# The first product of an attention kernel taken piece by piece over all row tiles, with joint query and key transfers and sixteen transposes ahead of it

## The chip, the cores and the metric

The kernel runs on one core of one Trainium2 chip, alone. The metric is the time of one execution in microseconds (us) as the device measures it; a kernel's time is the median of several executions. Lower is better.

## The reference, cut to what matters

The input x is (4, 512, 512) in float32. A first layer computes single-head attention over each of the four sequences, an MLP on its result and a second MLP on the result and the first MLP's output together; three further layers are adapters with weights chosen per sequence by an index, each with a residual and a layer norm. Only the attention is near the change:

```python
q = x @ Wq
k = x @ Wk
v = x @ Wv
attn = jnp.einsum('btd,bTd->btT', q, k) * scale
attn = jax.nn.softmax(attn, axis=-1)
attn_out = jnp.einsum('btT,bTd->btd', attn, v) @ Wp + bp
cms_out = jax.nn.gelu(attn_out @ cW1 + cb1, approximate=False) @ cW2 + cb2
```

## The kernel before, in words

**Arithmetic.** Each float32 operand is split into two parts for TensorE: a high part, which ScalarE makes by a cast to `fp32r`, and a low part, which VectorE makes by subtracting the high part from the operand. A product of two operands is then three matmuls (high by high, high by low, low by high) that accumulate in one PSUM bank: `mm3` (line 538). Its matmuls all stand on line 541 in the profile. Tiles are 128 rows; a 512 by 512 by 512 product has four row tiles `m` and four pieces `k` of the contraction, so 4 x 4 x 3 = 48 matmuls of 128x128 by 128x512, and each row tile has a PSUM bank of its own. `product` (line 545) goes over `m` outside and `k` inside; in the first row tile it calls `ready(k)`, which waits for the semaphore of piece `k`.

**Order of the work.** The kernel does not compute q and k. It forms G = Wq Wk^T once (`J_G`, into `g_w`) and for each sequence U = G x^T (`J_U0`, then per sequence), and scores from U and x. Likewise Wv Wp is formed once (`J_VP`). TensorE's program (lines 583 to 604) is: `J_G` in the upper four banks (`HIGH`), `J_U0` in the lower four (`LOW`), `J_VP` in the upper, `J_S0` (scores of sequence 0) in the lower; then for each sequence values (`v_jobs`), transposes of the probabilities (`pT_jobs`, line 572, by the identity in `ident`), probabilities by values, and U and scores of the next sequence. After that come the up and down products of the two MLPs (from line 606 on) and the three adapter layers.

**Loads at the front.** SyncE issues all transfers here (lines 364 to 375), in this order: for each `k` the query rows into `wq_raw` and the key rows into `wk_raw` (256 KB each, a semaphore each, line 366), x of sequence 0 into `res` (1 MB), the value and projection weights (1 MB each), four small ones, and the expert indices, whose values it then waits for and reads before it goes on (line 376).

**The splits at the front.** ScalarE (lines 809 to 812) waits for one transfer after the other and casts it into the high part of `wqT` or `wkT` (semaphore `qk_hi`); VectorE (lines 1127 to 1130) makes the low parts in the same order (`qk_split`). After the eight pieces ScalarE casts x, copies the four banks of `J_G` into the high parts of `g_w` as they fill (line 773) and casts the value and projection weights; VectorE makes the low parts in the same order (line 1072 for `g_w`), and then sums the betas of the later layers (`bsum`, line 1139).

**The prep pieces.** A second job goes along with the attention: the adapter weights (36 pieces) are loaded into three slots `prep`, cast by ScalarE (`piece_hi`, line 788, at places written out by hand between its other work), subtracted by GpSimd (line 1498) and stored in DRAM by SyncE (lines 389 to 404). In the first phase SyncE issues two loads and then waits for the sum of the betas (`bsum_store`, line 382) before the first store and the third load. The cast of the last piece of the first phase stands on ScalarE ahead of the exponentials of sequence 0 (line 793), and the first values of `v_jobs` wait for an exponential to release a bank.

**The identity.** GpSimd makes it at the start (lines 1483 to 1486); TensorE waits for it on line 590, after four products.

Of the kernel before, what the change touches and what calls it, by code (L numbers as in the profile page):

```python
# [8 lines left out]
ALU = mybir.AluOpType  # L9
# [3 lines left out]
P = 128  # L13
B = 4
S = 512
V = 512
# [4 lines left out]
DT = V // P  # L21
# [32 lines left out]
NRAW = 3  # L54
DSTEP = 8
GHL = 3


def chunk_of(ci):
# [36 lines left out]
    return tuple(n + LAYER_STEPS[l].index((i, part)) for i in (P4, P3))  # L96


def build(nc, wts, xin, bias_in, codes_in, experts_in, up_w, dn_w, wdu_all, pp_all, gb_all,
          bup_all, out):  # L100
    ctx = ExitStack()
    with ctx:
        base = -(-nc.sbuf_base // 64) * 64

        def at(name, kib, shape, dt=F32):

            return nc.alloc_sbuf_tensor_at(name, shape, dt, offset=base + int(kib * KiB))

        def sem(name):
            return ctx.enter_context(nc.semaphore(name))  # L110

        wqT = at("wqT", 0, [P, 2, DT, V], F32R)
        wkT = at("wkT", 16, [P, 2, DT, V], F32R)
# [7 lines left out]
        pT = at("pT", 144, [P, 2, DT, S], F32R)  # L121
        wp_s = at("wp_s", 144, [P, 2, DT, V], F32R)

        wq_raw, wk_raw, wv_raw, wp_raw = (at(f"w{n}_raw", 112 + 8 * i, [P, DT, V]) for i, n in enumerate("qkvp"))

        res = at("res", 160, [P, B, DT, S])
        probs = at("probs", 192, [P, DT, S])
# [10 lines left out]
        g = at("g", 128, [P, QC, 4, S])  # L138
        g_hl = [at(f"g_hl{i}", 144 + 4 * i, [P, 2, S], F32R) for i in range(GHL)]
        u_t, v_t, w_t = (at(n, k, [P, S]) for n, k in (("u_t", 156), ("v_t", 158), ("w_t", 204)))  # L140
# [15 lines left out]
        ident = at("ident", 206, [P, P])  # L156
        sm = at("sm", 206.5, [P, 224])
        NB_BIAS = 2 * HT + 3 * DT
        bias = sm[:, 0:NB_BIAS]
# [31 lines left out]
        bank = [psum[:, i, :] for i in range(BANKS)]  # L191
# [12 lines left out]
        def f(ap):  # L204

            return ap.bitcast(F32)
# [4 lines left out]
        qk_hi = sem("weights_qk_rows_hi_done")  # L211
        qk_split = sem("weights_qk_rows_split")
        x_hi = sem("x_transposed_hi_done")
        x_split = sem("x_transposed_split")
        s_wqk = [[sem(f"weight_{n}_rows_landed_{i}") for i in range(DT)] for n in ("q", "k")]
        s_x = sem("x_transposed_landed")
        s_small = sem("small_inputs_landed")
        s_idx = sem("experts_landed")
        s_ident = sem("identity_ready")
# [3 lines left out]
        bank_full = sem("bank_full")  # L223
# [78 lines left out]
        LOW, HIGH = 0, DT  # L302
        J_G, J_U0, J_VP, J_S0 = (DT * i for i in range(4))
# [58 lines left out]
        @block.sync  # L362
        def _(sp):
            for k in range(DT):
                for i, w in enumerate((wq_raw, wk_raw)):
                    sp.dma_start(w[:, k, :], wts[2 + i, :, k, :]).then_inc(s_wqk[i][k], 16)
            sp.dma_start(res[:, 0, :, :], xin[0]).then_inc(s_x, 16)
            for i, w in enumerate((wv_raw, wp_raw)):
                sp.dma_start(w[:, :, :], wts[i]).then_inc(s_w[i], 16)
# [19 lines left out]
            for phase in range(B):  # L389
                for c in range(PHASE + 2):  # L390
                    if c >= 2:
                        o = c - 2
                        i = o % PSLOT
                        sp.wait_ge(p_lo, phase * PHASE + (o + 1))
                        sp.dma_start(wdu_split[phase * PHASE + o], prep[i][:, :, :]).then_inc(p_free[i], 16)
                    if c < PHASE:
                        i = c % PSLOT
# [139 lines left out]
        def _(pe):  # L537
# [7 lines left out]
            def product(n, group, lhs, rhs, ready=None, free=None, tiles=range(DT)):  # L545

                for m in tiles:
                    if free is not None:
                        free(m)
                    elif ready is None or m > 0:  # L550
                        pe.wait_ge(dve_done, n + m - (BANKS - 1))
                    for k in range(DT):
                        if m == 0 and ready is not None:
                            ready(k)
                        ins = mm3(bank[group + m],
                                  lambda e: lhs[:, e, k, m * P:(m + 1) * P], lambda e: rhs[:, e, k, :],
                                  k == 0, k == DT - 1)
                    ins.then_inc(bank_full, 1)

            def split(sem_, before, per_k=1):  # L560

                return lambda k: pe.wait_ge(sem_, before + per_k * (k + 1))
# [17 lines left out]

                return lambda k: pe.wait_ge(dve_done, n + (k + 1) + (1 if k == DT - 1 else 0))

            product(J_G, HIGH, wqT, wkT, ready=split(qk_split, 0, per_k=2), free=known)
            pe.wait_ge(x_split, DT)
            product(J_U0, LOW, g_w, xT, ready=split(dve_done, J_G), free=known)
            pe.wait_ge(s_wsplit[0], 1)
            pe.wait_ge(s_wsplit[1], 1)
            product(J_VP, HIGH, wvT, wp_s)
            product(J_S0, LOW, uT, xT, ready=split(dve_done, J_U0))
            pe.wait_ge(s_ident, 1)  # L590
            for b in range(B - 1):
                n = b * PER
                v_jobs(n + JV, (0, 1, 2), ready=split(dve_done, J_VP))
# [63 lines left out]
            def down_chunk(ci):  # L657
                for d in range(DSTEP):
# [4 lines left out]
                    for m in range(DT):  # L663
                        if k == 0:
                            down_bank_free(ci, q, m)
                        mm3(bank[4 * q + m], lambda e: w_hl[k % 2][:, e, m * P:(m + 1) * P],
                            lambda e: g_hl[(DSTEP * ci + d) % GHL][:, e, :], k == 0, k == 3).then_inc(d_used, 1)

# [98 lines left out]
        def _(act):  # L767
# [39 lines left out]
                nc.scalar.copy((a_ops, c_ops)[s][i][:, 0, :, :], src).then_inc(op_hi[s], 1)  # L807

            for k in range(DT):
                for i, (w, raw_w) in enumerate(((wqT, wq_raw), (wkT, wk_raw))):  # L810
                    act.wait_ge(s_wqk[i][k], 16)
                    nc.scalar.copy(w[:, 0, k, :], raw_w[:, k, :]).then_inc(qk_hi, 1)
            x_hi_parts(0)
            hi_jobs(J_G, HIGH, lambda m: g_w[:, 0, m, :])
            for i, (w, raw_w) in enumerate(((wvT, wv_raw), (wp_s, wp_raw))):
# [8 lines left out]
            for b in range(B - 1):  # L824
                n = b * PER
# [84 lines left out]
            def g_hi(ci, d):  # L910
# [4 lines left out]
                if t >= GHL:  # L915
                    act.wait_ge(d_used, 4 * (t - GHL + 1))
                nc.scalar.copy(g_hl[t % GHL][:, 0, :], g[:, q, 2 * row + seq, :]).then_inc(g_hi_done, 1)  # L917

# [48 lines left out]
            for ci in range(NCH):  # L967
                p, l, c = chunk_of(ci)
                for q in range(QC):
                    for pos in range(len(LAYER_STEPS[l])):  # L970
                        n = aop_at(ci, q) + pos
# [94 lines left out]
        def _(dve):  # L1066
# [58 lines left out]
                    nc.vector.tensor_tensor((a_t4, c_t4)[s][:, :, :], b21, b11, ALU.subtract).then_inc(t_sum[s], 1)  # L1125

            for n in range(2 * DT):
                w, raw_w = ((wqT, wq_raw), (wkT, wk_raw))[n % 2]
                dve.wait_ge(qk_hi, n + 1)
                nc.vector.tensor_tensor(w[:, 1, n // 2, :], raw_w[:, n // 2, :], f(w[:, 0, n // 2, :]), ALU.subtract).then_inc(qk_split, 1)  # L1130
            x_lo_parts(0)
            lo_jobs(J_G, HIGH, g_w)
            for i, (w, raw_w) in enumerate(((wvT, wv_raw), (wp_s, wp_raw))):
# [18 lines left out]
            for b in range(B - 1):  # L1152
                n = b * PER
# [177 lines left out]
            for ci in range(NCH):  # L1331
                p, l, c = chunk_of(ci)
                for q in range(QC):
                    for pos in range(len(LAYER_STEPS[l])):
                        n = aop_at(ci, q) + pos
# [248 lines left out]
```

## Time and profile before

| | us |
|---|---|
| median of 3 runs | 1236.32 |
| lowest and highest run | 1235.46, 1237.90 |
| the profiled execution's own time | 1239.01 |
| its span, from the first instruction to the last | 1236.9 |
| TensorE busy in the span | 1191.9 |
| VectorE, ScalarE, GpSimd busy | 807.4, 567.0, 173.5 |
| mean granted TensorE clock in the span | 0.994 |

The span is the part of an execution that the profile shows instruction by instruction; what lies around it is in the execution's own time alone. Busy times of engines overlap. Ends of matmuls are modelled, so that spacings from start to start say more than durations. The row PEclk has the granted clock in tenths of full speed (9 stands for 90% or more); in a table by stretches it is a share of 1.00.

### The profile page before, as it was taken

What the parts mean: (1) busy time and instruction counts of PE and PEld (TensorE: products, weight loads), DVE (VectorE), ACT (ScalarE), POOL (GpSimd) and SP (SyncE); (2) the same over time, 40 slices, a digit from 0 to 9 for tenths busy, and PEclk for the clock granted to TensorE, in tenths of its full rate; (3) what the DMA queues carried; (4) which work ended last, traced back from release to release, by engine and by line L of the source; (5) the groups of instructions that cost most, each with busy time, mean ns of one, the idle gap of its engine ahead of it and who ended that gap; (6) DMA issues with size and microseconds to landing.
All of it is one profiled execution on the core that took longest, in us unless ns stands there. A gap on an engine that the chain in (4) does not pass through costs nothing.

```text
span 1236.9 us, 15228 instructions
## 1 busy us (share of the span) xinstructions
PE 1191.9 (96%) x5312; PEld 973.7 (79%) x5312; DVE 807.4 (65%) x1461; ACT 567.0 (46%) x1068; POOL 173.5 (14%) x147
## 2 busy tenths in 40 slices
PE   7999999799999899999999999989999999999997
PEld 5878878677788688888887787768888888788776
DVE  5444385746766766565766666686665565879986
ACT  5334353554533534343524633544343433266666
POOL 1332230000000000000000000000000000488871
PEclk9999999899999999999999999999999999999999
DMA  5755452114312202020461221411111118655534
GB/s 189 271 199 180 162 176 85 43 43 153 122 58 77 87 16 94 10 94 9 169 274 51 88 83 51 171 51 51 52 52 52 52 34 322 229 189 193 175 137 170
DMA packets 51186, 145.82 MB, mean 118 GB/s; under 512 B 6420, under 2 KB 6420, under 8 KB 46886
## 3 DMA queue, kind: packets, MB, share of 16 engines
q1 hardware_dynamic: 51110, 144.84, 33.2%
q8 instruction: 43, 0.70, 0.2%
q14 instruction: 33, 0.27, 0.1%
HBM read 108.11 MB, written 36.71 MB: 117 GB/s over the span
## 4 chain that ended last, share of the span: by engine, by line
PE 71%; DVE 11%; POOL 8%; ACT 4%; issue 4%; DMA 1%; SPq 0%; POOLq 0%; DVEq 0%; ACTq 0%
PE psum L541 70%; POOL res L1525 3%; POOL res L1527 3%; DVE ring L1187 1%; DMA prep<-wdu_dram 1%; ACT z L1016 1%; ACT ring L877 1%; POOL sm L1518 1%; DVE g_hl L1254 1%; DVE sm L1434 1%; DVE res L1269 1%; DVE res L1324 1%; DVE w_t L1228 0%; DMA wk_raw<-wts_dram 0%; POOL prep L1498 0%
## 5 line engine op out<-in xcount | busy, mean ns | idle before, releaser
L541 PE MATMUL psum<-g_hl,w_hl 128*128 128x512 f32 x1536 | 353.3, 390 | 1.5 <-DVE g L1242 1.3
L541 PE MATMUL psum<-a_op,ring 128*128 128x512 f32 x1344 | 324.4, 394 | 17.5 <-DVE w_t L1228 11.1
L541 PEld LDWEIGHTS psum<-g_hl,w_hl 128*128 128x128 f32 x1536 | 287.9, 188 | 64.6 <-DVE g L1242 4.8
L541 PEld LDWEIGHTS psum<-a_op,ring 128*128 128x128 f32 x1344 | 252.9, 190 | 77.8 <-DVE w_t L1228 14.5
L541 PE MATMUL psum<-c_op,ring 128*128 128x512 f32 x672 | 166.1, 394 | 0.6 <-DVE c_op L1296 0.6
L1254 DVE TENSOR_TENSOR g_hl<-g,g_hl 128x512 fp32r<-128x512 f32 x128 | 87.7, 691 | 111.7 <-ACT g_hl L917 110.4
L541 PEld LDWEIGHTS psum<-c_op,ring 128*128 128x128 f32 x672 | 127.3, 190 | 28.5 <-DVE c_op L1296 2.0
L1506 POOL TENSOR_TENSOR yT<-res,yT 128x512 fp32r<-128x512 f32 x8 | 11.7, 1487 | 875.6 <-ACT yT L1011 875.6
L877 ACT CAST ring<-asum 128x256 fp32r<-128x256 f32 x192 | 76.2, 403 | 122.3 <-PE psum L541 100.9
L917 ACT CAST g_hl<-g 128x512 fp32r<-128x512 f32 x128 | 78.3, 618 | 101.1 <-PE psum L541 101.1
L1187 DVE TENSOR_TENSOR ring<-asum,ring 128x256 fp32r<-128x256 f32 x192 | 80.8, 422 | 63.8 <-ACT ring L877 61.3
L894 ACT ACTIVATE g<-g,sm 128x512 f32<-128x512 f32 x96 | 69.6, 725 | 109.9 <-DVE g L1234 47.5
L1187 DVE TENSOR_TENSOR ring<-rawp,ring 128x256 fp32r<-128x256 f32 x144 | 60.8, 422 | 81.0 <-ACT ring L877 81.0
L1269 DVE TENSOR_TENSOR res<-psum,res 128x512 f32<-128x512 f32 x96 | 64.8, 691 | 24.1 <-PE psum L541 24.0
L877 ACT CAST ring<-rawp 128x256 fp32r<-128x256 f32 x144 | 57.0, 403 | 46.3 <-PE psum L541 46.2
L541 PE MATMUL psum<-yT,wd 128*128 128x512 f32 x288 | 68.6, 394 | 6.0 <-issue 6.0
L1498 POOL TENSOR_TENSOR prep<-prep 128x512 f32<-128x512 f32 x36 | 51.6, 1437 | 131.4 <-ACT prep L788 131.4
L541 PE MATMUL psum<-wu,h_hl 128*128 128x512 f32 x288 | 67.4, 390 | 0.0
L541 PEld LDWEIGHTS psum<-yT,wd 128*128 128x128 f32 x288 | 53.1, 188 | 18.0 <-issue 7.3
L541 PEld LDWEIGHTS psum<-wu,h_hl 128*128 128x128 f32 x288 | 54.0, 188 | 11.2
L1016 ACT ACTIVATE z<-z,sm 128x512 f32<-128x512 f32 x46 | 33.9, 808 | 37.7 <-DVE sm L1402 37.7
L1525 POOL TENSOR_TENSOR res<-z,bc 128x512 f32<-128x512 f32 x32 | 48.2, 1507 | 12.4 <-ACT z L1016 12.4
(124 smaller groups left out, 1381.2 us busy)
## 6 DMA issues: line engine op xcount, KB each, us to landing
rawp<-up_w_dram SPq DMA_DIRECT2D x48, 512.0 KB, 3.6
wdu_split<-prep SPq DMA_DIRECT2D x36, 512.0 KB, 2.9
wraw<-dn_w_dram SPq DMA_DIRECT2D x64, 256.0 KB, 3.1
wd<-wdu_split SPq DMA_DIRECT2D x12, 1024.0 KB, 7.3
wu<-wdu_split SPq DMA_DIRECT2D x12, 1024.0 KB, 5.4
prep<-wdu_dram SPq DMA_DIRECT2D x36, 256.0 KB, 3.3
second_pair_operands<-c_op SPq DMA_DIRECT2D x7, 1024.0 KB, 6.9
a_op<-second_pair_operands SPq DMA_DIRECT2D x7, 1024.0 KB, 11.3
```

What stands on the lines that cost most here:

```text
L541: ins = nc.tensor.matmul(ps, lw(el), rw(er), start=first and i == 0, stop=last and i == 2, skip_group_check=skip)
L877: nc.scalar.copy(ring[n % RING][:, 0, :], aop_src(n)).then_inc(aop_hi, 1)
L894: nc.scalar.activation(dst, src, ACT.Gelu, bias=(cb1, mb1)[l][:, t:t + 1]).then_inc(gelu_done, 1)
L917: nc.scalar.copy(g_hl[t % GHL][:, 0, :], g[:, q, 2 * row + seq, :]).then_inc(g_hi_done, 1)
L1016: nc.scalar.activation(z[u % 2][:, i, :], z[u % 2][:, i, :], ACT.Identity, scale=rstd[:, u % 2, i:i + 1], bias=nmr[:, u % 2, i:i + 1]).the ...
L1187: nc.vector.tensor_tensor(ring[n % RING][:, 1, :], aop_src(n), f(ring[n % RING][:, 0, :]), ALU.subtract).then_inc(aop_lo, 1)
L1254: nc.vector.tensor_tensor(g_hl[t % GHL][:, 1, :], g[:, q, 2 * row + seq, :], f(g_hl[t % GHL][:, 0, :]), ALU.subtract).then_inc(g_lo_done, 1)
L1269: nc.vector.tensor_tensor(dst, bank[4 * seq + m], dst, ALU.add).then_inc(d_evac, 1)
L1324: nc.vector.tensor_scalar(res[:, 2 + seq, m, :], res[:, 2 + seq, m, :], 0.0, 1.0, ALU.max, ALU.min).then_inc(y0_done, 1)
L1498: nc.gpsimd.tensor_tensor(prep[i][:, 1, :], prep[i][:, 1, :], prep[i][:, 0, :], ALU.subtract).then_inc(p_lo, 1)
L1525: nc.gpsimd.tensor_tensor(res[:, u % B, i, :], z[i2][:, i, :], bc[i2][:, 0, :], ALU.mult).then_inc(t_rmul, 1)
L1527: nc.gpsimd.tensor_tensor(res[:, u % B, i, :], res[:, u % B, i, :], bc[i2][:, 1, :], ALU.add).then_inc(t_res, 1)
```

## The change

In SyncE's program the eight transfers of query and key rows become four: piece `k` of both goes into `wqk_raw[:, k]`, whose layout in DRAM and in SBUF is partition, query or key, 512 values, so that 4 KB of a partition are contiguous. There is one semaphore per piece. ScalarE waits once per piece and casts the query part and then the key part; VectorE's subtractions read the new tile.

On TensorE the first product has a function of its own, `product_by_pieces`. It goes over `k` outside and `m` inside: for each piece it waits for both high parts, does the high by high matmul of all four row tiles, waits for both low parts, and does the two mixed matmuls of all four. The 48 matmuls are the same and write the same four banks. Ahead of it TensorE waits for the identity and transposes it sixteen times (`WARM`) into bank 0, which `J_U0` later overwrites. The wait for the identity further down is gone.

```diff
         def _(sp):
             for k in range(DT):
-                for i, w in enumerate((wq_raw, wk_raw)):
-                    sp.dma_start(w[:, k, :], wts[2 + i, :, k, :]).then_inc(s_wqk[i][k], 16)
+                sp.dma_start(wqk_raw[:, k, :, :], wqk[k]).then_inc(s_wqk[k], 16)
             sp.dma_start(res[:, 0, :, :], xin[0]).then_inc(s_x, 16)
...
-            product(J_G, HIGH, wqT, wkT, ready=split(qk_split, 0, per_k=2), free=known)
+            def product_by_pieces():
+
+                for k in range(DT):
+                    pe.wait_ge(qk_hi, 2 * k + 2)
+                    for m in range(DT):
+                        nc.tensor.matmul(bank[HIGH + m], wqT[:, 0, k, m * P:(m + 1) * P], wkT[:, 0, k, :], start=k == 0, stop=False)
+                    pe.wait_ge(qk_split, 2 * k + 2)
+                    for m in range(DT):
+                        for el, er in ((0, 1), (1, 0)):
+                            ins = nc.tensor.matmul(bank[HIGH + m], wqT[:, el, k, m * P:(m + 1) * P], wkT[:, er, k, :],
+                                                   start=False, stop=k == DT - 1 and el == 1)
+                        if k == DT - 1:
+                            ins.then_inc(bank_full, 1)
+
+
+            pe.wait_ge(s_ident, 1)
+            for i in range(WARM):
+                nc.tensor.transpose(bank[LOW][:, i % DT * P:(i % DT + 1) * P], ident[:, :], ident[:, :])
+            product_by_pieces()
             pe.wait_ge(x_split, DT)
             product(J_U0, LOW, g_w, xT, ready=split(dve_done, J_G), free=known)
             pe.wait_ge(s_wsplit[0], 1)
             pe.wait_ge(s_wsplit[1], 1)
             product(J_VP, HIGH, wvT, wp_s)
             product(J_S0, LOW, uT, xT, ready=split(dve_done, J_U0))
-            pe.wait_ge(s_ident, 1)
...
             for k in range(DT):
-                for i, (w, raw_w) in enumerate(((wqT, wq_raw), (wkT, wk_raw))):
-                    act.wait_ge(s_wqk[i][k], 16)
-                    nc.scalar.copy(w[:, 0, k, :], raw_w[:, k, :]).then_inc(qk_hi, 1)
+                act.wait_ge(s_wqk[k], 16)
+                for i, w in enumerate((wqT, wkT)):
+                    nc.scalar.copy(w[:, 0, k, :], wqk_raw[:, k, i, :]).then_inc(qk_hi, 1)
...
             for n in range(2 * DT):
-                w, raw_w = ((wqT, wq_raw), (wkT, wk_raw))[n % 2]
+                w = (wqT, wkT)[n % 2]
                 dve.wait_ge(qk_hi, n + 1)
-                nc.vector.tensor_tensor(w[:, 1, n // 2, :], raw_w[:, n // 2, :], f(w[:, 0, n // 2, :]), ALU.subtract).then_inc(qk_split, 1)
+                nc.vector.tensor_tensor(w[:, 1, n // 2, :], wqk_raw[:, n // 2, n % 2, :], f(w[:, 0, n // 2, :]), ALU.subtract).then_inc(qk_split, 1)
```

## Rows read from the trace of the kernel before

**Rows 1.** The page: TensorE's busy time, the granted clock in 40 slices, the chain.

```profile
PE 1191.9 (96%) x5312; PEld 973.7 (79%) x5312; DVE 807.4 (65%) x1461; ACT 567.0 (46%) x1068; POOL 173.5 (14%) x147
...
PEclk9999999899999999999999999999999999999999
...
PE 71%; DVE 11%; POOL 8%; ACT 4%; issue 4%; DMA 1%; SPq 0%; POOLq 0%; DVEq 0%; ACTq 0%
```

**Rows 2.** The chain in order of time, 0 to 60 us: start, duration, what.

```profile
3.07 5.98 DMA wk_raw<-wts_dram
...
10.47 47.09 PE psum L541 x198
```

**Rows 3.** Timeline, the first two products: start, duration, engine, line, operation, count, idle before.

```profile
6.23 1.65 PE L541 MATMUL psum<-wkT,wqT 128*128 128x512 f32 x3 [6.23 <-DVE wkT L1130]
...
10.47 11.71 PE L541 MATMUL psum<-wkT,wqT 128*128 128x512 f32 x42 [0.74 <-DVE wkT L1130]
...
22.02 11.04 PE L541 MATMUL psum<-xT,g_w 128*128 128x512 f32 x48
```

**Rows 4.** Stretches: length, PE, PEld, DVE, ACT, POOL, granted clock, DMA share, GB/s.

```profile
239.70:246.40 6.70, 5.51 (x13) 4.34 (x14) 6.21 (x10) 3.74 (x8) 0.00 (x0) 0.50 0.14 42
...
413.80:417.10 3.30, 3.30 (x10) 2.52 (x9) 2.71 (x9) 2.15 (x5) 0.00 (x0) 0.50 0.37 148
...
1229.50:1233.00 3.50, 2.16 (x16) 1.71 (x16) 1.73 (x4) 2.53 (x4) 0.40 (x1) 1.00 0.34 131
```

**Rows 5.** Timeline of TensorE inside two of these stretches.

```profile
240.89 5.49 PE L541 MATMUL psum<-a_op,ring 128*128 128x512 f32 x12 [4.70 <-DVE w_t L1228]
...
414.05 2.76 PE L541 MATMUL psum<-c_op,ring 128*128 128x512 f32 x6
416.61 0.63 PE L541 MATMUL psum<-a_op,ring 128*128 128x512 f32 x1
```

**Rows 6.** Two stretches of the front, columns as in rows 4.

```profile
2.50:8.50 6.00, 2.06 (x4) 1.25 (x5) 2.67 (x4) 3.07 (x5) 0.00 (x0) 1.00 0.93 286
11.00:15.00 4.00, 4.00 (x12) 2.86 (x11) 2.21 (x5) 2.13 (x5) 0.00 (x0) 1.00 1.01 428
```

**Rows 7.** Timeline: the identity and the first piece's splits.

```profile
1.17 0.29 POOL L1485 TENSOR_SCALAR_AFFINE_SELECT ident<-ident 128x128 f32<-128x128 f32 x1 [0.24 <-POOL ident L1483]
...
4.23 0.62 ACT L812 CAST wqT<-wq_raw 128x512 fp32r<-128x512 f32 x1 [2.23 <-DMA wq_raw<-wts_dram]
...
5.49 0.69 DVE L1130 TENSOR_TENSOR wkT<-wk_raw,wkT 128x512 fp32r<-128x512 f32 x1
```

**Rows 8.** Timeline: last tile of `g_w`, sum of betas, first prep pieces; then the page's prep loads.

```profile
21.43 0.83 SPq L399 DMA_DIRECT2D prep<-wdu_dram  x2
22.22 0.59 ACT L773 CAST g_w<-psum 128x512 fp32r<-128x512 f32 x1 [2.13 <-PE psum L541]
...
22.84 0.69 DVE L1072 TENSOR_TENSOR g_w<-psum,g_w 128x512 fp32r<-128x512 f32 x1 [2.03 <-ACT g_w L773]
...
27.51 4.49 POOL L1498 TENSOR_TENSOR prep<-prep 128x512 f32<-128x512 f32 x2 [25.81 <-ACT prep L788]
...
29.06 1.78 DVE L1139 TENSOR_TENSOR bsum<-bsum,bsum 6x512 f32<-6x512 f32 x1
...
prep<-wdu_dram SPq DMA_DIRECT2D x36, 256.0 KB, 3.3
```

**Rows 9.** Timeline: transposes of probabilities, and the last transposes of the kernel.

```profile
62.83 1.91 PE L575 MATMUL psum<-ident,probs 128*128 128x128 f32 x16
...
1231.00 1.75 PE L748 MATMUL psum<-ident,z 128*128 128x128 f32 x14 [0.66 <-ACT z L1016]
```

**Rows 10.** Timeline: where ScalarE's prep casts meet TensorE's stream.

```profile
52.25 0.62 ACT L788 CAST prep<-prep 128x512 fp32r<-128x512 f32 x1 [2.41 <-DMA prep<-wdu_dram]
...
54.66 8.34 PE L541 MATMUL psum<-vp_w,xT 128*128 128x512 f32 x36
...
67.99 11.55 PE L541 MATMUL psum<-pT,v_n 128*128 128x512 f32 x48 [0.50 <-DVE pT L1072]
```

More of the change, by code:

```diff
@@ L56 @@
 GHL = 3
+WARM = 16
 def chunk_of(ci):
@@ L96, in raw_done, with build @@
     return tuple(n + LAYER_STEPS[l].index((i, part)) for i in (P4, P3))
-def build(nc, wts, xin, bias_in, codes_in, experts_in, up_w, dn_w, wdu_all, pp_all, gb_all,
+def build(nc, wqk, wts, xin, bias_in, codes_in, experts_in, up_w, dn_w, wdu_all, pp_all, gb_all,
           bup_all, out):
@@ L122, in build @@
         wp_s = at("wp_s", 144, [P, 2, DT, V], F32R)
-        wq_raw, wk_raw, wv_raw, wp_raw = (at(f"w{n}_raw", 112 + 8 * i, [P, DT, V]) for i, n in enumerate("qkvp"))
+        wqk_raw = at("wqk_raw", 112, [P, DT, 2, V])
+        wv_raw, wp_raw = (at(f"w{n}_raw", 128 + 8 * i, [P, DT, V]) for i, n in enumerate("vp"))
         res = at("res", 160, [P, B, DT, S])
@@ L214, in build @@
         x_split = sem("x_transposed_split")
-        s_wqk = [[sem(f"weight_{n}_rows_landed_{i}") for i in range(DT)] for n in ("q", "k")]
+        s_wqk = [sem(f"weights_qk_rows_landed_{i}") for i in range(DT)]
         s_x = sem("x_transposed_landed")
@@ L1552 @@
     wts = np.stack([rows(a["L0_cond_" + n]) if n == "Wp" else rows(a["L0_cond_" + n].T)
-                    for n in ("Wv", "Wp", "Wq", "Wk")])
+                    for n in ("Wv", "Wp")])
+    wqk = np.stack([a["L0_cond_" + n].T.reshape(DT, P, V) for n in ("Wq", "Wk")], axis=2)
     m_up = np.stack([up_pieces(a["L0_cond_mW1"][:V]), up_pieces(a["L0_cond_mW1"][V:])], axis=1)
@@ L1569 @@
     arrays = {
-        "wts": wts, "x": np.stack([rows(a["x"][b].T) for b in range(B)]), "bias": bias,
+        "wqk": wqk, "wts": wts, "x": np.stack([rows(a["x"][b].T) for b in range(B)]), "bias": bias,
         "codes": a["itok_B_17_1546"].reshape(1, B), "experts": a["itok_B_1_2"].reshape(1, B),
```

## The prediction

> **What bounds the kernel now.** I read the page first: TensorE is busy for 96% of the span, and of the chain that ended last it has 71% [rows 1]. So the kernel is bound by the matmul stream, and a change at the front is worth what it moves the whole stream forward, unless something later takes that back. The chain in order of time says where the front is bound: a transfer of key rows until 9.05 us, a cast, a subtraction, and then 47 us of matmuls without a break from 10.47 [rows 2]. The timeline of TensorE says how those first microseconds look [rows 3]. The first product (48 matmuls) starts at 6.23 with three matmuls, waits, does three more, waits, and is only continuous from 10.47, because the first row tile needs all four pieces before the second tile may start. It ends where the next product (`J_U0`) starts, at 22.02; I call that moment E. The 48 matmuls of that next product take 11.04 us with the longer tail of the last one, 0.227 from one start to the next, 10.9 in all.
>
> **Two speeds.** The first three matmuls take 1.65 us [rows 3], which is what six take at full speed (48 take 11.04). The clock row of the page says 9 from the start, so it can't be used for the first microseconds; I go by spacing. In a stretch with granted clock 0.50 six matmuls start in 2.56 us (414.05 to 416.61), 0.427 each [rows 4, 5]. That is the 1.2 GHz level, 0.227 is the 2.4 GHz level. How long was the slow level at the front? From 10.47 to 22.02 there are 42 matmuls in 11.55 us; at full speed they would take 9.53; the excess of 2.02 is bought at 1 - 0.227/0.427 = 0.47 us per us, so the clock rose some 4 us after the engine had become continuous. The other case in the trace: continuous from 240.89 after an idle time of 4.7 us, and 0.50 until 246.4, so 5.6 us [rows 4, 5]. I use 4 to 5.6 us.
>
> **The change part by part.**
>
> *Transfers.* Eight issues of 256 KB become four of 512 KB, with 4 KB per partition in one stretch where there were 2 KB. In 2.5 to 8.5 us the row pieces moved at 286 GB/s, in 11 to 15 us, with 8 KB stretches, the rate was 428 [rows 6]. For 4 KB I bound by the two and take 350: a piece of 512 KB every 1.5 us (1.83 at the lower rate). The first query piece is in at 4.2, its cast starts at 4.23, and the key piece is in by the end of that cast [rows 7]; so the first joint piece lands between 4.2 and 4.85, I take 4.5. Two casts of 0.62 and a subtraction of 0.69 follow [rows 7]: high parts ready at 4.5 + 1.3 = 5.8, all parts at 6.5. The fourth piece lands at 9.0 (10.3 at the lower rate), its last part is ready at 11.0 (12.3). SyncE issues four fewer transfers of 0.43 us; the x, value and projection rows behind them come up to 1.5 us earlier, or unchanged; neither is waited for (the chain does not go over them).
>
> *The order of the first product.* With pieces outside and row tiles inside, each piece feeds 12 matmuls: 2.7 us at full speed, 5.1 at the slow one. Pieces come every 1.5 to 1.83 us, so after the first piece TensorE never waits. It runs from 5.8 in one go: E = 5.8 + 48 x 0.227 = 16.7 at full speed. The last piece alone would allow 11.0 + 2.7 = 13.7 (15.0 at the late bound), so data don't end last. Each microsecond at the slow clock after 5.8 adds 0.47.
>
> *Price of that order.* All four banks now fill in the last 1.4 us instead of one each 2 to 3 us. Before, three of the four copies and subtractions of `g_w` lay beside matmuls, and only the last showed: cast at 22.22, subtraction at 22.84 [rows 8]. Now ScalarE starts tile 0 at E - 1.2, VectorE ends it at E + 0.1, and then one tile each 0.7 us. The next product needs a new tile each 3 x 0.227 = 0.68 us, so it starts 0.2 late and just keeps pace. The fourth cast starts 0.4 later against E than before and VectorE is free 0.7 later; the weight splits and the sum of the betas (29.06 to 30.84 [rows 8]) stand behind them in order, so I set them 0.5 later against E.
>
> *Transposes of the identity.* The identity is ready at 1.46 [rows 7]. Sixteen transposes of the probabilities take 1.91 us, 0.12 each at full speed [rows 9]. At the slow level no row shows them; an estimate is twice that, 3.8 us, so from 1.5 to 5.3. The first high parts are ready at 5.8, so they cost nothing as such; the cover is 0.5 us, and were it gone each 0.1 us more would put E later by no more than that. The ends of that price: 0.12 each, or 0.80 each if nothing overlapped, as 1.65 us for three matmuls less two spacings leaves 0.80 for a single slow one. I take the estimate, since the nearest row shows transposes overlapped. What they may bring is the clock. If they count as work, the engine is nearly continuous from 1.5, and the clock rises at 5.5 to 7.1: E = 16.7 to 17.3, I take 17.0. If not, it rises 4 to 5.6 after 5.8: E = 18.6 to 19.3, I take 18.9. Do they count? At the end of the kernel, from 1229.5 to 1233, TensorE ran nothing but 16 transposes, 14 of them from 1231.0 on, busy for 2.16 of 3.5 us, and the granted clock of that stretch is 1.00 [rows 4, 9]. That speaks for it, but for holding a clock, not for raising one.
>
> The Trainium skill, "TensorE: Matmul & The Clock Gate", section "Part 4: PE-mode transpose", says the full clock "doesn't engage for transpose-mode". By that rule the sum would take E = 18.9, the first rival below. The rows of the kernel's end lean against it, and none tests it for a rise.
>
> *What follows.* The queue that could hold the rest is that of the `prep` pieces (SyncE load, ScalarE cast, GpSimd subtraction, store). Its stores start when the betas are summed, so it moves by 22.0 - 17.0 - 0.5 = 4.5. Its first two loads are issued at 21.43 [rows 8], behind the value loads of the experts, and come 0 to 1.5 earlier with the transfers. At 0 the first piece lands at 24.7 (3.3 after its issue), is cast in 0.62 and subtracted in some 2.2 (two of them take 4.49 [rows 8]), and the first store could go at 27.5, where it now has to wait for the sum of the betas at 30.84: a shift of 3.3; at 1.5 it would be 4.8, and no bound. I take 4.3, nearer to the second, since the transfers in front of those loads do get shorter. That matters, since this queue touches the stream twice: the cast of the last piece at 52.25 stands ahead of the exponentials that free the banks for 54.66, and the matmuls at 67.99 wait 0.50 for the transposed probabilities behind such a piece [rows 10]. So the gain is that of the queue, 4.3, not the 4.8 of TensorE.
>
> *Sum.* 4.3 us off the profiled execution (1239.0) is 1234.7; its span, 1236.9, is as long as the median of the runs, 1236.3, and the median less 4.3 is 1232.0. A measurement of this kernel can tell about 0.2% (2.5 us) from no change.
>
> **The rivals.** (1) *The transposes don't raise the clock.* E = 18.9, gain 22.0 - 18.9 - 0.5 = 2.6, time 1233.7. For it: no row shows a rise from transposes, and they leave a gap of about 0.5 us before the product. Against it: the clock that held at the end. 0.28. (2) *The piece queue eats it.* If the `prep` loads don't move and each cast then waits for its load, ScalarE, which has the exponentials and the casts of the transposed probabilities behind them, keeps only a part: gain 1 to 2, time 1234.8. For: the zero slack at 67.99. Against: the queue is started anew by the betas, which move with TensorE. 0.15. (3) *The front is bound by data anyway*, the larger transfers landing later or the product waiting for them: gain under 1, time 1235.8. Against: the 3.0 us between 13.7, which the last piece allows, and the 16.7 of 48 matmuls. 0.06. (4) *The transposes hold the first product back.* If they don't overlap in the slow state, 16 x 0.80 = 12.8 puts the product's start at 14.3 and E at 25.2: 3.2 us later, plus 0.5 behind it, time 1240.0. It decides from 0.56 us per transpose (start 10.5, E 21.4). For: no row at this clock. Against: at full speed they overlap, 0.12 each. 0.05.
>
> **How the numbers follow.** Forecast, 4.3: 0.46. Its own range is 3.3 (loads unmoved) to 5.0 (data early, clock up at once), 1231.3 to 1233.0; medians of three lie about 1 us off (the runs spread from 1235.5 to 1237.9). So the low end is 1230.2. Upward rivals 1 and 2 have to be in, with the same 1 us: 1236.4. Faster by over 0.2%: nearly all of the forecast (0.45), over half of rival 1 (0.16), a little of 2 (0.03): 0.64. Slower: rival 4 and 0.02 for a sum of small things: 0.07. Same: 0.29.
>
> **What would show it.** Right: matmuls of the first product in one row of 48 from about 5.8, spacing 0.23 from 7 us or before, the second product starting at 17 to 17.3, and the matmuls now at 54.66 and 67.99 some 4.3 us earlier. Wrong: slow spacing until 10 (rival 1), a longer wait at pT or an exponential behind a cast that waits for a load (rival 2), waits for wkT inside the product (rival 3), transposes beyond 6 us (rival 4). The forecast falls if the shift at 22 us is not found again at the end of the attention.

## The result, and the profile after

The changed kernel takes 1233.14 us (median of 7 runs, 1231.82 to 1235.85); the kernel before, measured beside it, 1238.71 (median of 7, 1235.46 to 1239.85). The ratio is 0.996, with a 95% interval of 0.9946 to 0.9974: about 4.9 us faster, 3.2 to 6.7 by the interval (the two medians lie 5.6 apart). The profiled execution went from 1239.01 to 1233.20 us, its span from 1236.9 to 1231.2.

From the page of the changed kernel: TensorE's busy time is what it was, and it has less of the chain, where VectorE, ScalarE and transfers have more [rows 1].

```profile
PE 1192.0 (97%) x5328; PEld 975.0 (79%) x5328; DVE 806.3 (65%) x1461; ACT 566.3 (46%) x1068; POOL 171.3 (14%) x147
...
PE 68%; DVE 12%; POOL 8%; ACT 5%; issue 3%; DMA 2%; SPq 0%; POOLq 0%; ACTq 0%; DVEq 0%
```

The timeline of the changed kernel's front (start, duration, engine, line, operation, count, idle before):

```profile
1.52 3.33 PE L601 MATMUL psum<-ident 128*128 128x128 f32 x16 [1.52 <-POOL ident L1503]
...
4.42 0.62 ACT L830 CAST wqT<-wqk_raw 128x512 fp32r<-128x512 f32 x1 [2.40 <-DMA wqk_raw<-wqk_dram]
...
5.61 1.20 PE L589 MATMUL psum<-wkT,wqT 128*128 128x512 f32 x4 [0.76 <-ACT wkT L830]
...
6.64 2.02 PE L593 MATMUL psum<-wkT,wqT 128*128 128x512 f32 x8
...
8.50 1.07 PE L589 MATMUL psum<-wkT,wqT 128*128 128x512 f32 x4
...
14.85 1.98 PE L593 MATMUL psum<-wkT,wqT 128*128 128x512 f32 x8
15.51 2.06 ACT L791 CAST g_w<-psum 128x512 fp32r<-128x512 f32 x4 [2.58 <-PE psum L593]
16.12 2.49 DVE L1090 TENSOR_TENSOR g_w<-psum,g_w 128x512 fp32r<-128x512 f32 x4 [2.23 <-ACT g_w L791]
...
16.96 11.13 PE L542 MATMUL psum<-xT,g_w 128*128 128x512 f32 x48
```

Beside rows 3: there the first product began with three matmuls in 1.65 us, at the slow level, and was continuous from 10.47. Here the first four take 1.20, near the 1.07 that four take later at full speed, and from 5.61 there is no further wait; the second product starts at 16.96 where it was 22.02. Sixteen transposes take 3.33 us; spaced 0.213 at first, the last three 0.11 to 0.12 apart, so the clock rose at 4.4 us, while nothing but transposes had run. (The clock column has 1.00 before the first rise in every trace here, so I read every first rise from the spacing of starts.)

Two stretches of the changed kernel, columns as in rows 4: where the pieces land, and one further on.

```profile
4.60:8.00 3.40, 2.64 (x13) 2.00 (x12) 2.93 (x5) 3.13 (x6) 0.00 (x0) 1.00 1.05 428
...
407.20:410.50 3.30, 3.30 (x9) 2.55 (x8) 2.71 (x8) 1.95 (x4) 0.00 (x0) 0.50 0.56 204
```

The chain of the changed kernel in order of time, 0 to 64 us:

```profile
15.51 2.06 ACT g_w L791 x4
17.56 1.81 ACT wvT L835
19.39 2.29 DVE wvT L1153
21.68 2.20 DVE wp_s L1153
23.88 1.71 DVE bsum L1157
...
26.00 0.34 SPq L396
...
26.39 3.49 DMA prep<-wdu_dram
...
56.32 4.12 DMA prep<-wdu_dram
...
61.61 2.48 DVE pT L1090 x4
```

The same from 56 us on:

```profile
64.75 15.26 PE psum L542 x66
```

Where rows 2 had one stretch of matmuls from 10.47 to 57.56, TensorE is off the chain from 15.5 to 64.7 us. The chain goes through the copies of `g_w`, the weight splits and the sum of the betas into the prep queue and along it to the transposed probabilities. The queue's first store went from 31.26 to 26.00.

The gain along the kernel, before less after: 5.1 us at the second product (22.02 to 16.96), 5.0 at the values (54.66 to 49.69), 5.6 at the probabilities' product (67.99 to 62.37, where the wait of 0.50 is gone), 6.0 at the matmul before which the kernel before waits for `uT` (the tenth of its product, 184.59 to 178.57), 5.7 to the end (1236.9 to 1231.2).

### The profile page after: what moved, and what is told of

Read it like the earlier page. It is cut to its first block, busy times and chain, and to the rows that moved or that the text cites. A ratio compares the mean times of both kernels' runs of the same rounds, so it can differ in the third digit from the quotient of the medians.

```text
span 1231.2 us, 15256 instructions
## 1 busy us (share of the span) xinstructions
PE 1192.0 (97%) x5328; PEld 975.0 (79%) x5328; DVE 806.3 (65%) x1461; ACT 566.3 (46%) x1068; POOL 171.3 (14%) x147
## 4 chain that ended last, share of the span: by engine, by line
PE 68%; DVE 12%; POOL 8%; ACT 5%; issue 3%; DMA 2%; SPq 0%; POOLq 0%; ACTq 0%; DVEq 0%
PE psum L542 67%; POOL res L1543 3%; POOL res L1545 3%; DMA prep<-wdu_dram 2%; DVE ring L1205 1%; ACT z L1034 1%; ACT ring L895 1%; POOL sm L1536 1%; DVE g_hl L1272 1%; POOL prep L1516 1%; DVE sm L1452 1%; DVE res L1342 1%; DVE w_hl L1265 1%; DVE res L1287 1%; DVE w_t L1246 0%
## 5 line engine op out<-in xcount | busy, mean ns | idle before, releaser
L542 PE MATMUL psum<-a_op,ring 128*128 128x512 f32 x1344 | 324.7, 394 | 17.6 <-DVE w_t L1246 11.1
L1516 POOL TENSOR_TENSOR prep<-prep 128x512 f32<-128x512 f32 x36 | 49.1, 1371 | 128.0 <-ACT prep L806 128.0
## 6 DMA issues: line engine op xcount, KB each, us to landing
a_op<-second_pair_operands SPq DMA_DIRECT2D x7, 1024.0 KB, 11.9
```

Of the source, the lines that this page charges most:

```text
L542: ins = nc.tensor.matmul(ps, lw(el), rw(er), start=first and i == 0, stop=last and i == 2, skip_group_check=skip)
L1516: nc.gpsimd.tensor_tensor(prep[i][:, 1, :], prep[i][:, 1, :], prep[i][:, 0, :], ALU.subtract).then_inc(p_lo, 1)
```

## The experiments

Gains are one less the ratio to the kernel before, times 1237. "Second" is the start of the second product, "probabilities" that of the product in the last line of rows 10.

| kernel | product starts | clock rises | second | probabilities | ratio (95%) |
|---|---|---|---|---|---|
| before | 6.23 | 14.4 | 22.02 | 67.99 | 1 |
| changed | 5.61 | 4.4 | 16.96 | 62.37 | 0.9960 (0.9946 to 0.9974) |
| changed, once more | 5.53 | 6.2 | 17.11 | 63.21 | 0.9956 (0.9938 to 0.9974) |
| no transposes | 5.79 | 8.7 | 18.44 | 63.85 | 0.9977 (0.9966 to 0.9987) |
| eight transposes | 5.56 | 10.6 | 19.25 | 65.03 | 0.9986 (0.9977 to 0.9994) |
| 32 transposes | 7.51 | 6.7 | 18.80 | 65.23 | 0.9981 (0.9972 to 0.9991) |
| separate transfers | 5.45 | 5.8 | 17.35 | 63.80 | 0.9965 (0.9954 to 0.9977) |
| transposes alone | 6.27 | up, down at 8.6, up at 15.4 | 22.67 | 68.64 | 0.9996 (0.9987 to 1.0006) |
| order alone | 5.56 | 9.9 | 18.91 | 64.34 | 0.9976 (0.9966 to 0.9986) |
| joint transfers alone | 6.35 | 11.9 | 19.98 | 65.26 | 0.9972 (0.9964 to 0.9981) |
| queue late | 5.68 | 5.9 | 17.07 | 66.82 | 0.9994 (0.9984 to 1.0004) |
| queue early | 5.68 | 9.4 | 18.73 | 64.12 | 0.9957 (0.9943 to 0.9970) |
| twenty transposes | 5.86 | 4.6 | 17.22 | 62.62 | 0.9956 (0.9940 to 0.9971) |
| twenty, queue early | 5.70 | 7.5 | 17.83 | 64.06 | 0.9957 (0.9942 to 0.9971) |

The columns of starts and rises come from one profiled execution each, the ratio from all runs. The intervals reach about 1 to 2 us to either side, so that the ratio tells apart only gains that differ by more than that.

### No transposes

```diff
-WARM = 16
+WARM = 0
```

> The changed kernel with no transposes ahead of the first product (joint transfers and the piece-by-piece order stay). Theory (order and clock each give a part): the product starts at 5.6 us as before, at the 1.2 GHz level, spaced 0.427 us; the clock rises 4 to 5.6 us later, so the second product starts at 18.9 to 19.6 us where it is 16.96 in the changed kernel, and the whole is 1.9 to 2.6 us slower than the changed kernel, about 3 us faster than the kernel before. Rival (the transposes do nothing for the clock, which would have risen anyway): second product at 17.0 us, no difference from the changed kernel.

```profile
5.79 2.04 PE L589 MATMUL psum<-wkT,wqT 128*128 128x512 f32 x4 [5.79 <-ACT wkT L830]
7.63 2.50 PE L593 MATMUL psum<-wkT,wqT 128*128 128x512 f32 x8
...
18.44 11.13 PE L542 MATMUL psum<-xT,g_w 128*128 128x512 f32 x48
```

Gain 2.8 us. Four matmuls take 2.04 us where they took 1.20: the product starts slow, as the theory has it, and the rival is out. The clock rose 2.9 us after the engine became continuous, sooner than the 4 to 5.6 of the kernel before, so the second product is only 1.5 us later than in the changed kernel, under the range expected. The transposes are worth 1.3 to 1.5 us at the second product (18.44 less 17.11 or 16.96), and by the ratios some 2 us of the whole (4.9 less 2.8), with intervals that overlap.

### Transposes alone

```diff
+            pe.wait_ge(s_ident, 1)
+            for i in range(WARM):
+                nc.tensor.transpose(bank[LOW][:, i % DT * P:(i % DT + 1) * P], ident[:, :], ident[:, :])
             product(J_G, HIGH, wqT, wkT, ready=split(qk_split, 0, per_k=2), free=known)
```

> The kernel before with the sixteen transposes ahead of the first product, and nothing else. Theory (the clock is worth something only if the product then runs on without waits): the clock rises at 4.4 us, the product starts at 6.2 and waits for its second, third and fourth piece until 11.9 us, being busy for a third of that time; the clock falls back in between and the second product starts at 21.5 to 22.3 us, no gain over the kernel before (22.0). Rival (the clock, once up, stays up over these waits): 39 matmuls at 0.227 us from 11.9, second product at 20.8 us, gain 1.3 us.

The timeline of TensorE, and a stretch inside it:

```profile
1.52 3.67 PE L586 MATMUL psum<-ident 128*128 128x128 f32 x16 [1.52 <-POOL ident L1488]
6.27 0.96 PE L542 MATMUL psum<-wkT,wqT 128*128 128x512 f32 x3 [1.08 <-DVE wkT L1133]
8.85 1.65 PE L542 MATMUL psum<-wkT,wqT 128*128 128x512 f32 x3 [1.62 <-DVE wkT L1133]
10.70 12.13 PE L542 MATMUL psum<-wkT,wqT 128*128 128x512 f32 x42 [0.20 <-DVE wkT L1133]
22.67 11.04 PE L542 MATMUL psum<-xT,g_w 128*128 128x512 f32 x48
```

```profile
8.70:15.40 6.70, 6.35 (x14) 4.22 (x15) 4.33 (x8) 4.46 (x9) 0.00 (x0) 0.50 1.02 427
```

The three matmuls of the first piece take 0.96 us: the clock was up. Those of the second take 1.65 again, and from 8.7 to 15.4 the granted clock is 0.50. Between, the engine had waited for pieces most of the time. The clock was won and lost again, and the gain is 0.5 us with zero inside its interval. The theory holds in this: the transposes pay only where the product then runs on. The second product, at 22.67, is 0.65 later than in the kernel before and outside the 21.5 to 22.3 expected.

### Order alone

```diff
-            product(J_G, HIGH, wqT, wkT, ready=split(qk_split, 0, per_k=2), free=known)
+            product_by_pieces()
```

> The kernel before with the first product piece by piece over all four row tiles, and nothing else (eight separate transfers, no transposes). Theory: the product starts at 5.5 us and never waits; slow for 4 to 5.6 us, then fast: second product at 18.4 to 19.2 us, 2.8 to 3.6 us earlier than in the kernel before, and the whole faster by 2.5 to 4 us. Rival (the separate transfers hold the product): waits for wkT inside the product, second product after 20 us.

```profile
5.56 2.07 PE L588 MATMUL psum<-wkT,wqT 128*128 128x512 f32 x4 [5.56 <-ACT wkT L827]
7.44 3.15 PE L592 MATMUL psum<-wkT,wqT 128*128 128x512 f32 x8
...
18.91 11.15 PE L541 MATMUL psum<-xT,g_w 128*128 128x512 f32 x48
```

Second product at 18.91, gain 3.0 us, both as expected; no wait inside the product. With separate transfers the data do not hold it.

### Joint transfers alone

```diff
-                for i, w in enumerate((wq_raw, wk_raw)):
-                    sp.dma_start(w[:, k, :], wts[2 + i, :, k, :]).then_inc(s_wqk[i][k], 16)
+                sp.dma_start(wqk_raw[:, k, :, :], wqk[k]).then_inc(s_wqk[k], 16)
```

> The kernel before with the joint transfers and nothing else (old order, no transposes). Theory: the pieces' low parts are ready at 6.4, 7.7, 8.9 and 10.2 us, each feeds three slow matmuls of 0.43 us, so that the first row tile has hardly a wait left and the engine is continuous from 6.4 us on; slow for 4 to 5.6 us, second product at 19.2 to 20 us, 2 to 2.8 us before the 22.0 of the kernel before. Rival (transfers alone are worth nothing, as I costed them): continuous only from 9 to 10 us, second product at 21 to 22 us, gain under 1 us.

```profile
6.35 13.79 PE L542 MATMUL psum<-wkT,wqT 128*128 128x512 f32 x48 [6.35 <-DVE wkT L1131]
19.98 11.04 PE L542 MATMUL psum<-xT,g_w 128*128 128x512 f32 x48
```

One line of 48 matmuls without a wait: the pieces come as fast as three slow matmuls use them up, and the old order has nothing left to wait for. Second product 2.0 us earlier, whole 3.5 us faster. My costing of the transfers at nothing holds, and only nearly, beside the new order. Alone, each of the two makes the product continuous, and the second to come finds most of that already done: 3.0 and 3.5 us of the whole alone, 2.8 together (no transposes), which the intervals don't tell apart; at the second product 3.1 and 2.0 alone, 3.6 together.

### Separate transfers under the other two edits

```diff
-                sp.dma_start(wqk_raw[:, k, :, :], wqk[k]).then_inc(s_wqk[k], 16)
+                for i, w in enumerate((wq_raw, wk_raw)):
+                    sp.dma_start(w[:, k, :], wts[2 + i, :, k, :]).then_inc(s_wqk[i][k], 16)
```

> The changed kernel with the eight separate transfers of the kernel before (transposes and piece-by-piece order stay). Theory: the clock rises during or just behind the transposes, the product starts at 5.5 and never waits for a piece, and the second product starts at 16.8 to 17.3 us, as in the changed kernel (16.96). But the expert indices land 2.8 us later at the end of the longer row of transfers, so the first two prep loads are issued at 21.4 instead of 18.8, the first store goes at 26.5 instead of 26.0, and the probabilities' product starts 0.5 to 1 us later than the 62.37 of the changed kernel. Whole: 0.5 to 1 us slower than the changed kernel, 4 to 4.5 faster than the kernel before. Rival (the joint transfers carry a real part of the gain beside the other two): a wait for wkT in the product and a second product after 18 us.

```profile
17.35 11.14 PE L542 MATMUL psum<-xT,g_w 128*128 128x512 f32 x48 [0.57 <-DVE g_w L1090]
...
63.80 11.53 PE L542 MATMUL psum<-pT,v_n 128*128 128x512 f32 x48 [0.90 <-DVE pT L1090]
```

The product never waits for a piece, but the second product waits 0.57 us for `g_w`, and the probabilities 0.90 us behind the prep queue: 1.4 us later than in the changed kernel's first trace, 0.6 later than in its second (63.21). Gain 4.3 us; the intervals overlap with the changed kernel's, so the whole tells nothing between them. The traces lean to the joint transfers: neither trace of the changed kernel has that wait for `g_w`, and the prep loads are issued at 18.8 in both, at 22.2 here.

### Queue late

```diff
+            bsum_store()
             for phase in range(B):
                 for c in range(PHASE + 2):
...
                     if c == XPOS:
-                        if phase == 0:
-                            bsum_store()
-                        else:
+                        if phase:
                             x_next(phase)
```

> The changed kernel with the wait for the sum of the betas (and its store) ahead of the first two prep loads instead of behind them; nothing else, and TensorE's front is not touched. Theory (the prep queue has no slack against TensorE's stream, so that it sets the gain): the first two loads are issued at 26 instead of 18.8 us, the queue runs some 5 us later, the values' product at 49.7 waits for the exponentials by 2 to 3.5 us, and the probabilities' product starts at 66 to 67.5 instead of 62.37; the whole is 4 to 5 us slower than the changed kernel, that is, no faster than the kernel before. Rival (the queue has slack, TensorE alone sets the gain): under 1 us of difference at 62.4 and in the whole.

The timeline of TensorE:

```profile
38.92 11.04 PE L541 MATMUL psum<-xT,uT 128*128 128x512 f32 x48
52.05 8.48 PE L541 MATMUL psum<-vp_w,xT 128*128 128x512 f32 x36 [2.10 <-ACT probs L810]
...
66.82 3.80 PE L541 MATMUL psum<-pT,v_n 128*128 128x512 f32 x9 [1.81 <-DVE pT L1089]
```

TensorE's front is the same (second product at 17.07), and all of it is given back: 2.10 us before the values, for the exponentials that stand behind the queue's last cast, and 1.81 before the probabilities' product. In this trace the clock then fell as well:

```profile
67.40:70.70 3.30, 3.30 (x9) 2.62 (x8) 3.30 (x6) 3.26 (x8) 0.04 (x1) 0.50 0.71 238
```

Gain over the kernel before 0.7 us, interval across zero, against 4.9. The first store went at 29.70 instead of 26.00, and the two waits together are 3.9 us: the queue has no slack to lose.

### Eight and 32 transposes

```diff
-WARM = 16
+WARM = 8
```

> The changed kernel with eight transposes instead of sixteen. They end at 3.2 us and leave TensorE idle for 2.4 us. Theory (what raises the clock is that the engine runs on nearly without a break into the product): no early rise, the product runs slow from 5.6 and the second product starts at 18.4 to 19.3 us as without transposes; 1.5 to 2.3 us slower than the changed kernel. Rival (some transposes are enough, how many does not matter): clock up by 5.6 us, second product at 17.0.

> The changed kernel with 32 transposes instead of sixteen. Theory: 14 at 0.213 us until the clock rises at 4.4, the rest at 0.109, so they end at 6.4 to 6.6 us, where the first high parts were ready at 5.6; the first product and the second start 0.8 to 1 us later (second at 17.8 to 18), and the whole is 0.8 to 1 us slower than the changed kernel. If the clock rises only at 7 to 8 us, all 32 are slow, end at 8.3 and cost 2.7. Rival (the later transposes run beside the product and cost nothing): second product at 17.0.

TensorE with eight, then with 32 (`WARM = 32`):

```profile
1.52 1.97 PE L601 MATMUL psum<-ident 128*128 128x128 f32 x8 [1.52 <-POOL ident L1503]
5.56 2.08 PE L589 MATMUL psum<-wkT,wqT 128*128 128x512 f32 x4 [2.07 <-ACT wkT L830]
```

```profile
1.52 6.23 PE L601 MATMUL psum<-ident 128*128 128x128 f32 x32 [1.52 <-POOL ident L1503]
7.51 1.18 PE L589 MATMUL psum<-wkT,wqT 128*128 128x512 f32 x4
```

Eight leave 2.07 us idle, the product starts slow, and the gain is 1.7 us: no more than without any. With 32 the clock rose at 6.7, between the two cases that I had written down, so the transposes end at 7.5 and hold the product for 1.9 us; gain 2.4, about half of what sixteen give and no more than without any (2.8).

### The changed kernel once more, and the queue early

The first has no edit. The second moves SyncE's wait for the betas and VectorE's sum:

```diff
-                    if c == XPOS:
+                    if c == (XPOS if phase else 2):
...
             lo_jobs(J_G, HIGH, g_w)
+            dve.wait_ge(s_bsum_in, 32)
+            nc.vector.tensor_tensor(bsum[1][0:NS, :], bsum[1][0:NS, :], bsum[0][0:NS, :], ALU.add).then_inc(s_bsum, 1)
```

> The changed kernel itself, once more, unchanged. Theory: where the clock rises differs from execution to execution (4.4 us in the changed kernel's trace, 5.2, 5.8 and 5.9 in three traces of kernels with the same sixteen transposes), and none of these is late enough to cost more than 0.3 us at the second product: it starts at 16.9 to 17.3 us. The ratio to the kernel before is 0.995 to 0.997. Rival (the first trace had luck with the clock): rise after 7 us, second product after 17.6.

> The changed kernel with the sum of the betas ahead of the two weight subtractions on VectorE, and with SyncE's wait for it behind the first store and the third prep load instead of ahead of them. Theory (in the changed kernel the queue has just no slack, but TensorE's stream has none either): the first store goes at 25.1 instead of 26.0 us, the queue's casts come 0.5 to 0.9 us earlier, the probabilities' product starts at 62.2 to 62.4 where it was 62.37, since TensorE has no wait there to lose, and the wait of 0.28 us for uT at 177 goes; the whole is 0 to 0.5 us faster than the changed kernel. Rival (the queue still holds the stream back): product at 61.5, whole 1 us or more faster.

The changed kernel again: clock up at 6.2, second product 17.11, ratio 0.9956. One difference to its first trace: the probabilities' product starts at 63.21 after a wait of 0.54 us that the first trace did not have. The stretch around 407 us, which in the rows of the first trace above has 0.50, at the same place of the work here:

```profile
407.00:410.40 3.40, 3.38 (x15) 2.77 (x16) 2.93 (x8) 1.80 (x4) 0.00 (x0) 1.00 0.77 272
```

The kernel with the queue early did not test its theory cleanly: in its profiled execution the clock rose only at 9.4, in spite of sixteen transposes, and the second product started at 18.73. Its first store went at 26.84, not at the 25.1 expected. Its whole is as fast as the changed kernel (0.9957).

### Twenty transposes, without and with the queue early

```diff
-WARM = 16
+WARM = 20
```

> The changed kernel with twenty transposes instead of sixteen. With sixteen the engine is idle from 4.9 us to 5.5 or 5.7, and in one of seven traces with sixteen (the kernel with the queue early) the clock rose only at 9.4 us. Theory (that gap is what lets the rise fail): twenty transposes, all slow, end at 5.8 us, so that the engine has no gap at all before the product; the clock is up by 7 us in this trace, the product starts at 5.6 to 5.9, the second product at 17.0 to 17.6. Whole: same as the changed kernel within 0.5 us, ratio to before 0.995 to 0.9965. Rival (the late rise has nothing to do with the gap): rise after 8 us is as likely as before, second product at 18 to 18.8.

> The changed kernel with twenty transposes and with the prep queue started before the sum of the betas is waited for (both edits of the two kernels before together). Theory: second product at 17.0 to 17.6 us, first store at 25.1 to 25.5, no wait of TensorE before the probabilities' product (0.54 us in the second trace of the changed kernel), which starts at 62.4 to 62.9; whole 0.3 to 0.7 us faster than the changed kernel, ratio to before 0.9945 to 0.996. Rival (nothing left in the queue): same as the changed kernel with a wait of 0.3 to 0.6 us still there.

(The text says one of seven traces with sixteen; there are six.) Rises at 4.6 and 7.5, second products at 17.22 and 17.83, ratios 0.9956 and 0.9957. With the queue early the wait before the probabilities is still there:

```profile
64.06 11.30 PE L542 MATMUL psum<-pT,v_n 128*128 128x512 f32 x47 [0.68 <-DVE pT L1090]
```

So its rival holds. Against the second product the first store was sooner than in the changed kernel (8.1 us after it, 25.93 less 17.83, where that has 9.0), and the wait is still there. What the wait goes with is the time that one load takes. ScalarE's last prep cast before the probabilities' product, in the kernel before, in the two traces of the changed kernel, and here:

```profile
66.10 0.62 ACT L788 CAST prep<-prep 128x512 fp32r<-128x512 f32 x1 [2.48 <-DMA prep<-wdu_dram]
60.47 0.62 ACT L806 CAST prep<-prep 128x512 fp32r<-128x512 f32 x1 [1.83 <-DMA prep<-wdu_dram]
61.33 0.62 ACT L806 CAST prep<-prep 128x512 fp32r<-128x512 f32 x1 [2.53 <-DMA prep<-wdu_dram]
62.18 0.62 ACT L806 CAST prep<-prep 128x512 fp32r<-128x512 f32 x1 [2.65 <-DMA prep<-wdu_dram]
```

The product starts 1.9 us behind this cast in all four. The load in front of it was issued at 56.32, 56.45 and 56.37 in the last three, and the cast began 4.1, 4.9 and 5.8 us later; why the same load takes longer in one execution than in another was not found.

Neither twenty transposes nor the early queue can be told from the changed kernel, and no kernel here beats it by more than the intervals allow. Nor do these two test what the gap does. In the first the clock rose inside the transposes, so they ended early and left a gap of 0.44 us before the product; in the second there was no gap at all, and the rise at 7.5 is later than in five of the six traces with sixteen and a gap. Its second product, 17.83, is outside the 17.0 to 17.6 expected.

## Why the prediction was right

**Bound, and size.** A shift at the front was to go through to the end: it did, 5.1 us at 17 us and 5.7 at the end. These two traces can be compared at their ends, since both have the granted clock at 0.50 at the same two later places (413.80 in rows 4 and 830.2 before, 407.20 and 823.6 after). Forecast 1232.0 and a gain of 4.3 with an own range of 3.3 to 5.0; measured 1233.14 beside a kernel before that was itself 1238.71 in these runs, gain 4.9 by the ratio. The interval of the ratio holds the forecast; the 5.6 between the medians does not lie in its own range. The time alone would not decide: 1233.14 is nearer to the 1233.7 of rival 1 than to 1232.0, and it is the trace and the experiments that tell them apart.

**The order** (E = 16.7 at full speed): eight spacings of 0.227 from the 14.85 of the product's last line end at 16.7, and the second product began 0.3 later (16.96), where I had 0.2. The product started at 5.61 for the 5.8 of the working, with no wait inside. That 17.0 was met to 0.04 is in part luck: the clock rose before the product, and the working had it rise at 5.5 to 7.1. The second trace, with its rise at 6.2 and 17.11, is the case that was worked out.

**The transfers** were sized too slow. I took 350 GB/s between rows 6's two rates; the joint pieces moved at 428 GB/s, the rate of the 8 KB stretches, and the casts of the pieces followed each other every 1.3 us, not 1.5. With the new order that changed nothing at the first product, as worked out. That they are worth nothing at all was wrong as a statement about the edit: alone they gave 3.5 us, and under the other two 0.2 to 0.4 us at the second product and 0.6 to 1.4 at the probabilities, by one trace against two.

**The transposes** at the slow level: estimate 0.24 each, 3.8 us, measured 0.213 apart, 3.33 to 3.67 for the sixteen. They cost nothing, as worked out, and they raised the clock: the forecast's case. The 4 to 5.6 us of work before a rise were too narrow, having been taken from two cases: the clock rose 2.8 us after the first transpose in the changed kernel, 2.9 after the first matmul without transposes, and 6.0 after the first of twenty transposes with the queue early, with no gap before it. Rival 1 is out as a rule: in the changed kernel the spacing of the transposes themselves drops from 0.213 to 0.11 at 4.4 us. The sentence of the Trainium skill, "TensorE: Matmul & The Clock Gate", section "Part 4: PE-mode transpose", that full clock does not engage for transposes, is not what these traces show (4.4, and 4.6 with twenty). What is left of that rival is its time: it was the outcome of one execution in six with sixteen transposes (rise at 9.4, second product at 18.73), and rival 1 had 18.9 plus 0.2.

**The queue** was the term that I took as setting the gain, at 4.3. The mechanism holds: the chain now goes over it, and the late queue took the gain away. The size was off (so was the 4.8 set beside it for TensorE, which has no sum of its own: 22.0 less 17.0 is 5.0). The first store stands behind the sum of the betas, and both moved by 5.3 us (31.26 to 26.00, 29.06 to 23.80), not by 4.3. The prep loads, issued 2.6 us earlier (21.43 to 18.84) where I allowed 0 to 1.5, were no bound. The 0.5 that I charged for the shared copies of `g_w` was too much: the weight casts followed at once, and the betas moved by more than the 5.1 of TensorE. And the queue did not hold the gain under TensorE's: the probabilities' product moved by 5.6 us in the first trace and by 4.8, with the wait of 0.54, in the second, beside 5.1 and 4.9 at the second product.

**Rival 2** (the queue eats it) did not happen, but its condition is near: in one trace of the changed kernel the wait before the probabilities is 0, in the other 0.54. **Rival 3** fell with the waits inside the product gone. **Rival 4** fell with 0.213 us per transpose; its other half, that transposes can hold the product, is real at 32.

## What to carry to other kernels

Reordering a first product so that each arriving piece feeds all output tiles, and making its transfers larger, both cure the same thing, so don't add the two: alone they gave 3.0 and 3.5 us here, together 2.8 (3.1, 2.0 and 3.6 at the second product). Dummy work on TensorE ahead of the data paid here (1.3 to 1.5 us at the second product, some 2 of the whole) where it ended just before the data came and the engine then ran on; with waits behind it the clock was lost again, and with eight or 32 instead of sixteen the kernel was no faster than with none. After a gain at the front, look at the side queues that start from there: here one with no slack could have eaten all of it.

## What the runs showed that I had not expected

The clock falls later in the kernel, and where it does differs between executions of one kernel: from 407 us the granted clock is 0.50 in one trace of the changed kernel and 1.00 in the other, at about the same place of the work. In the first of these, nine matmuls touch a stretch of 3.3 us, in the second fifteen one of 3.4 us. What such a stretch costs can be read from two groups of matmuls that both traces have, one on each side of it (first the first trace, then the second):

```profile
401.55 1.67 PE L542 MATMUL psum<-a_op,ring 128*128 128x512 f32 x6 [1.34 <-ACT u_t L919]
413.59 5.60 PE L542 MATMUL psum<-a_op,ring 128*128 128x512 f32 x24
```

```profile
402.17 1.66 PE L542 MATMUL psum<-a_op,ring 128*128 128x512 f32 x6 [1.36 <-ACT u_t L919]
412.63 5.60 PE L542 MATMUL psum<-a_op,ring 128*128 128x512 f32 x24
```

The second trace is 0.6 us behind at the first group and 1.0 ahead at the second: the stretch costs 1.6 us, as 3.4 us do at the 0.47 us per us of the prediction. So the ends of two traces can only be compared with these stretches counted. The profiled execution without transposes took 1231.74 us, less than the changed kernel's 1233.20, though its second product starts 1.5 later: around 407 and 823 us, where the changed kernel's trace has a granted clock of 0.50, it has 1.00. Two such stretches, 3.2 us, are a part of the spread that the kernels show on one chip (before: 1233.7 to 1240.1 in 14 runs); that they are the whole cause was not tested.

The first rise, too, comes at different times with the same sixteen transposes: 4.4, 5.8, 5.9, 6.2 and 9.4 us in five traces, two of them of one kernel, that all run on into the product. What decides this was not found.
